# Self-attention: the second score tile of the next head pair behind three quarters of P times V, and the second piece of the first tile's transposes ahead of the second tile's maxima

## The reference

```
q = (x @ wq).reshape(B, S, 16, 64)        # B = 4, S = 1024; k and v likewise
scores = jnp.einsum('bqhd,bkhd->bhqk', q, k) + bias
weights = softmax(scores, axis=-1)
context = jnp.einsum('bhqk,bkhd->bqhd', weights, v).reshape(B, S, 1024)
return context @ wo
x = layernorm(x + attention(x))           # cross-attention and experts follow
```

## Time and profile before

| | us |
|---|---|
| median of three runs | 4514.3 |
| the profiled execution | 4509.74 |
| its span, first to last instruction | 4507.9 |
| PE busy in the span | 3896.7 (86%) |
| DVE busy in the span | 2494.0 (55%) |
| ACT busy in the span | 1579.7 (35%) |

### The profile page before, as it was taken

One profiled execution on the slowest core, in us unless ns is written; L12 is line 12 of the kernel. 1 busy time (PEld: TensorE's weight loads), 2 busy tenths in 40 slices (PEclk: granted clock), 3 DMA queues, 4 the chain that ended last, 5 costly groups with the idle time before them and its releaser, 6 DMA issues. The chain is left out here.

```text
span 4507.9 us, 90480 instructions
## 1 busy us (share of the span) xinstructions
PE 3896.7 (86%) x36730; PEld 2344.8 (52%) x36730; DVE 2494.0 (55%) x4793; ACT 1579.7 (35%) x3181; POOL 905.4 (20%) x1012
## 2 busy tenths in 40 slices
PE   5999887889998878899988788999987829999992
PEld 3767444547674445476643454766535504444441
DVE  3777335767773357577733676777236762222224
ACT  2444125744441257344413573444136700000000
POOL 2333101113330011133300112333001102222220
PEclk8999998999999999999999899999998969999996
DMA  8333258633332686333326853333178514444545
GB/s 261 93 88 88 85 222 297 207 110 88 88 88 85 240 294 201 101 88 93 83 85 260 287 188 101 94 92 93 71 281 282 171 59 106 127 123 110 139 112 168
DMA packets 285607, 659.36 MB, mean 146 GB/s; under 512 B 23920, under 2 KB 90144, under 8 KB 281968
## 3 DMA queue, kind: packets, MB, share of 16 engines
q1 hardware_dynamic: 269776, 616.08, 42.4%
q0 software_dynamic: 15120, 35.46, 4.1%
q10 hardware_dynamic: 320, 2.23, 0.1%
HBM read 384.84 MB, written 210.11 MB: 132 GB/s over the span
## 5 line engine op out<-in xcount | busy, mean ns | idle before, releaser
L493 ACT ACTIVATE sc<-sc,nmax 128x1024 f32<-128x1024 f32 x512 | 586.9, 1147 | 774.0 <-DVE nmax L712 773.2
L457 POOL TENSOR_SCALAR sc<-sc,pinv 128x1024 f32<-128x1024 f32 x512 | 574.6, 1122 | 1254.4 <-DVE pinv L720 1242.4
L824 DVE CUSTOM_DVE_ANT_0 sc<-psum,big 128x896 f32<-128x896 f32 (+7 forms) x512 | 373.4, 748 | 215.3 <-PE psum L1163 177.1
L988 PE MATMUL psum<-pts,wct 32*64 32x256 f32 x8192 | 465.6, 381 | 28.2 <-PEq L983 28.2
L988 PE MATMUL psum<-xall,wct 32*64 32x256 f32 x8192 | 466.1, 381 | 0.0
L962 PE MATMUL psum<-xt,w_all 128*128 128x256 f32 x1792 | 415.7, 385 | 15.6 <-PEq L959 15.6
L493 ACT ACTIVATE sc<-sc,xmax 128x896 f32<-128x896 f32 (+7 forms) x512 | 394.4, 772 | 70.0 <-DVE xmax L824 64.9
L730 DVE STREAM_TRANSPOSE pts<-sc 128x1024 f32<-128x1024 f32 (+3 forms) x352 | 333.0, 946 | 135.4 <-PE psum L988 92.4
L962 PEld LDWEIGHTS psum<-xt,w_all 128*128 128x128 f32 x1792 | 332.5, 190 | 120.4 <-issue 56.0
L988 PEld LDWEIGHTS psum<-pts,wct 32*64 32x64 f32 x8192 | 312.2, 134 | 131.2 <-issue 75.2
L712 DVE CUSTOM_DVE_ANT_0 sc<-psum,table_a 128x1024 f32<-128x1024 f32 x256 | 309.3, 1208 | 123.3 <-PE psum L972 106.3
(11 more groups left out here) (158 smaller groups left out, 5580.6 us busy)
## 6 DMA issues: line engine op xcount, KB each, us to landing
wct<-xall SPq DMA_DIRECT2D x576, 128.0 KB, 2.4
big<-skew_d SPq DMA_DIRECT2D x48, 1024.0 KB, 5.4
w_sb<-w_dram SPq DMA_DIRECT2D x48, 1024.0 KB, 6.3
big<-skew_d SPq DMA_DIRECT2D x48, 768.0 KB, 4.4
big<-skew_d SPq DMA_DIRECT2D x32, 896.0 KB, 4.6
big<-skew_d SPq DMA_DIRECT2D x32, 640.0 KB, 5.3
w_all<-wqkv_dram SPq DMA_DIRECT2D x33, 512.0 KB, 3.5
skew_d<-wct SPq DMA_DIRECT2D x8, 2048.0 KB, 6.9
```

The costliest lines, as they stand in the source:

```text
L457: pool.tensor_scalar(sc[k % 4][:, :], sc[k % 4][:, :], pinv[:, k % 4:k % 4 + 1], 1.0, ALU.mult, ALU.mult).then_inc(probs_scaled, 1)
L493: act.activation(tile, tile, ACT.Exp, bias=least, scale=-1.0, accum_out=total).then_inc(probs_ready, 1)
L824: dve.tensor_tensor_reduce(scx[u % 2][:, at], SCORES[:, at], skw[u % 4][:, at], -XSCALE, BIG, ALU.add, ALU.min, xmax[:, k:k + 1]).then_inc ...
L988: mm = pe.matmul(OSUM[HEAD[h], a, :], v_all[rows, ST * (b % GROUPS) + b // GROUPS, HEAD[h]], ptf[h][rows, QG * b:QG * b + QG], start=(b == ...
```

## The change

On PE, `weigh(1)` moves ahead of `score(1)` of the next pair; on DVE the second pieces of the turns of tile 0, one per head, move ahead of the two `add_bias` of tile 1. No instruction is added or removed.

```
@@ add_biases(), VectorE
                     invert_sum(0, 1)
                     turn(0, 0, 0, WEIGHED[1])
                     turn(0, 1, 0, WEIGHED[1])
+                    turn(0, 0, WEIGHED[1], WEIGHED[2])
+                    turn(0, 1, WEIGHED[1], WEIGHED[2])
                     add_bias(1, 0)
                     add_bias(1, 1)
                     invert_sum(1, 0)
                     invert_sum(1, 1)
-                    turn(0, 0, WEIGHED[1], WEIGHED[2])
-                    turn(0, 1, WEIGHED[1], WEIGHED[2])
                     turn(1, 0, 0, WEIGHED[2])
                     turn(1, 1, 0, WEIGHED[2])
@@ attend(), TensorE
                     weigh(0)
+                    weigh(1)
                     if more:
                         score(1, 1 - which)
-                    weigh(1)
                     weigh(2)
```

## The result

The changed kernel takes 4558.16 us (median of four runs, 4555.11 to 4562.7) against 4513.47 for the kernel before, with the four runs of it on the same chip. The ratio is 1.0099, with a 95% interval from 1.0084 to 1.0115: slower by 38 to 52 us. The forecast was 4555.5, that is 41.2 above before; 44.7 were measured. In a second round of runs it was 4553.38 (five runs), against 4514.9 for the kernel before: 38.5 above, ratio 1.0089 [1.0075, 1.0104].

What follows compares the result with a forecast made beforehand. PE was taken as the bound, busy 51.86 of 52.00 us a pair; 39.8 + 1.4 = 41.2 us on a median of 4514.3 gave 4555.5 us, likeliest case 4543 to 4564, 8 in 10 4540 to 4578.

Steps and rivals of the forecast that it cites:

- (a): On PE, weigh(1) ahead of score(1) makes score(1) start 3.46 us late; score(2) does not wait.
- (b): On DVE, the moved pieces of tile 0's turns fit into its wait for score(1), gaining 0.69 us behind.
- (c): POOL's scaling of tile 1 holds DVE's turn of head 1, 3.23 us late; 0.46 of the 0.69 is not had.
- (d): On DVE, both idle times are eaten and tile 2's maxima start at 346.99 instead of 345.29, 1.70 us late.
- (e): On PE, score(3) starts at about 349.45, some 1.5 us idle; score(4) 1.66 us late, about 0.3 idle.
- (f): From score(4) on, PE takes 5.63 us a tile, DVE 5.18; nothing comes back, 1.66 us lost at each boundary.
- rival of a delay taken up: DVE regains 0.45 us a tile from score(4) on, so nothing is lost: 4514 to 4517 us; chance 9%.
- (g): Six of seven boundaries in four items pay, 24 x 1.66 = 39.8 us; the one with PE's jump back costs nothing.
- (h): First pair of a batch item: 0.46 us stays, hidden in the first item; 3 x 0.46 = 1.4 us.
- rival of the clock: PE's clock falls behind the new idle times at each boundary, slowing scores and fillers: 4590 to 4630 us; chance 8%.

Runs made afterwards that it cites:

- PE half alone: Kernel before with only weigh(1) moved ahead of score(1) on PE, DVE's order as before: 4556.81 us, ratio 1.0089.
- filled order: Changed kernel with last pieces of tile 0's turns put between the turns of tile 1 on DVE: 4550.8 us, ratio 1.0082 against the kernel before.
- delay of 1.73 us: Kernel before with the first part of P times V cut at 20 blocks instead of 16, so score(1) stands 1.73 us late: 4516.92 us, ratio 1.0000.
- DVE half alone: Kernel before with only tile 0's second turn pieces moved ahead of tile 1's maxima on DVE, PE's order as before: 4587.34 us, ratio 1.0154.

## Why the prediction was right

- (a) score(1) 3.46 us late, score(2) on time: measured 342.91 - 330.45 = 12.46 behind score(0), where 337.61 - 325.14 = 12.47 was written, and score(2) at 18.02 as before.
- (b) The moved pieces fit ahead of tile 1's maxima, with 1.00 us to spare. The PE half alone shows what they bring: 0.19 us, not 0.69.
- (c) POOL binds the turn of head 1. It started at 350.13 - 5.31 = 344.82 in the time of the earlier trace rows, as written. The first turn was held a little too (348.98, which is 0.27 behind the last inversion's start instead of 0.08); that was not in the prediction and changed nothing here, since the turn of head 1 waits for POOL all the same. The filled order shows the wait was on the path.
- (d) Tile 2's maxima: 352.33 - 5.31 = 347.02, written 346.99. The delay of 1.73 us, which cost nothing and left DVE no idle time there, shows the budget that the two idle times made.
- (e) score(3) at 349.47 and score(4) at 354.66, written 349.45 and 354.61.
- (f) Nothing came back: 5.63 us a tile on PE behind score(4). The rival of a delay taken up is out.
- (g) 24 boundaries at 1.70 us instead of 1.66, 20 of them read from the pairs' lengths; the jump's boundary free, as the kernels with the loop written out show. In the last pair the delay carried through: from its score(0) to its score(5) it took 33.0 us before and 34.7 to 34.8 after, with the same idle times of 1.22 and 3.20 us at scores 5 and 6.
- (h) The first pair of items 2 to 4 was 0.46 to 0.49 us longer (from 50.13, 50.14 and 50.11 to 50.60 each), written 0.46; that of the first item was not longer (78.92 us before, 77.03 and 78.63 after). Its rows in the second item, the turn of head 1 held by POOL, and 2.21 behind it tile 2's maxima, for the earlier trace rows:

```profile
986.83 0.98 DVE L730 STREAM_TRANSPOSE xall<-sc 128x768 f32<-128x768 f32 x1 [0.17 <-POOL sc L457]
...
989.04 1.18 DVE L712 CUSTOM_DVE_ANT_0 sc<-psum,table_a 128x1024 f32<-128x1024 f32 x1
```

The term that was mis-sized is the cost of a boundary, 1.70 for 1.66: 24 x 1.70 + 1.4 = 42.2 us. That lies inside both measured intervals (38 to 52, and 34 to 47). The totals alone, 44.7 and 38.5, would not tell 41 from 35; it is the lengths of the pairs and the starts in them that bear the account out.

The rival of the clock is out as well. At the 24 boundaries of each profile of the changed kernel the tile of score(3) came behind 1.30 to 1.45 us of idle and took 1.99 us, at the full clock. Longer idle times at that score, up to 1.64 us in the PE half alone and up to 1.84 us in the DVE half alone, left it at 1.99 us too. Behind 1.98 us three tiles of four took 2.55 to 2.83 us, and behind the 2.6 to 3.2 us at the jump and in the last pairs it went either way. The prediction went by the nearest row it had (1.22 us) and was right in that; the margin, as far as these runs show it, was about 0.5 us of idle time. The Trainium skill ("TensorE: Matmul & The Clock Gate", section "HAM oscillation — how this bites in real kernels") tells of a kernel in which PE waits about 3 to 5 us for data between groups of matmuls and each next group starts at the lower level, in every pass. Here such a fall came already behind shorter idle times, and not in every pass.

The jump back cost PE an idle time of 2.70 to 3.20 us in the changed kernel, and it was gone with the loop written out. The Trainium skill's page "Runtime: NRT & Kernel Launch", section "Instruction fetch mechanics", says that a taken branch whose target is not among the instructions already fetched has to wait for their fetch. The runs agree with that as far as they show the idle time come and go with the jump; the fetch itself no run here shows.

## What to carry to other kernels

Where one engine is busy almost without a gap (here 0.14 us of idle in a pair), moving its work about can win next to nothing; what matters is how far the engine that feeds it runs ahead. Add up that engine's idle times along the chain that ends in the wait (here 1.33 us, with what the shorter pieces give): in these runs a delay up to about that sum cost nothing, and beyond it each us was paid each time round. When an instruction leaves such a chain, ask which engine is next late behind it: here POOL kept 0.5 of 0.69 us.

## What the runs showed of the hardware that I had not expected

- Writing out PE's loop removed four idle times of 2.7 to 3.2 us and the slow tiles behind them, 14.8 us at four boundaries, and the total stayed the same (ratio 0.9998). In the profile the other stages were 20.8 us longer, a good half of it PE's busy time; at one place a store ended later (a wait of 4.26 instead of 2.51 us) and the matmuls behind it ran at half the clock. The cause is open.
- A score tile behind an idle time of 2.7 to 3.2 us took anything from 1.99 to 3.79 us at the same place of the program: at the jump, 2.70 us of idle were followed by 1.99 us in one profile of the changed kernel (third item) and by 3.78 in the other (fourth item). Two profiles of this kernel differ by 12.5 us.
- The shortest idle time with a slow tile behind it, at this score, was 1.98 us; up to 1.84 us none was slow.
- Most pairs repeat to 0.02 us within a profile and between profiles, so a cost of 0.04 us a pair could be read there, where the intervals of the totals of 4515 us are 4 to 8 us wide to each side.
